# Two depthwise convolutions with group norms: border rows written three times, fetched with one transfer per half, and all bands of the second convolution ahead of its border products

## The reference

```python
# first layer: 5x5, 3x3 and 1x1 depthwise convolutions of the group-normed x, mixed by alpha
g = _gn(x)            # 32 groups of 3 channels, over 3*128*128 points of an image
x = x + alpha[0]*g + alpha[1]*dw1x1(g, w1) + alpha[2]*dw3x3(g, w3) + alpha[3]*dw5x5(g, w5)
# second layer: one 3x3 kernel for every channel, and a bias
g = _gn(x)
x = x + conv3x3(g, w) + b
```

## Time and profile before

| | |
|---|---|
| median of 3 runs | 431.48 us (428.29, 431.50, 431.48) |
| the profiled execution's own time | 432.64 us, of which the span in the trace is 430.8 us |
| mean granted clock of PE | 0.903 of full speed |
| busy in the span: PE, PE weight loads | 318.5 us (74%), 276.8 us (64%) |
| DVE, ACT, POOL | 318.1 us (74%), 304.1 us (71%), 262.3 us (61%) |
| DMA | 69.40 MB, mean 161 GB/s |
| chain that ended last, by engine | DVE 33%, DMA 21%, SP's queue 13%, ACT 13%, PE 9% |

### The profile page before, as it was taken

One profiled execution on the slowest core, in us unless ns is written; L12 is line 12 of the kernel. 1 busy time (PEld: TensorE's weight loads), 2 busy tenths in 40 slices (PEclk: granted clock), 3 DMA queues, 4 the chain that ended last, 5 costly groups with the idle time before them and its releaser, 6 DMA issues.

```text
span 430.8 us, 12547 instructions
## 1 busy us (share of the span) xinstructions
PE 318.5 (74%) x5206; PEld 276.8 (64%) x5206; DVE 318.1 (74%) x688; ACT 304.1 (71%) x372; POOL 262.3 (61%) x206
## 2 busy tenths in 40 slices
PE   2491586754986998679894998499848989898440
PEld 2361273643986798459883897389836989897220
DVE  7861899971886998399929994889649996779620
ACT  1407257089999699939995899759993999977320
POOL 6405055058788578827885588738882788865601
PEclk9997596995999899969996999889998999999685
DMA  6689488201687769676986788676868514731965
GB/s 151 169 174 204 129 188 169 73 3 41 159 200 164 199 177 210 158 189 202 199 194 171 198 184 202 161 214 173 189 163 223 145 41 118 201 97 28 264 173 146
DMA packets 112829, 69.40 MB, mean 161 GB/s; under 512 B 4540, under 2 KB 109892, under 8 KB 112772
## 3 DMA queue, kind: packets, MB, share of 16 engines
q1 hardware_dynamic: 106088, 65.31, 60.5%
q10 hardware_dynamic: 6684, 3.29, 3.3%
HBM read 41.10 MB, written 27.48 MB: 159 GB/s over the span
## 4 chain that ended last, share of the span: by engine, by line
DVE 33%; DMA 21%; SPq 13%; ACT 13%; PE 9%; issue 4%; ACTq 2%; POOL 2%; POOLq 0%; DVEq 0%
DVE xt L697 15%; DVE stats L641 13%; DMA xt<-in_x_dram 10%; PE ps L377 8%; DMA edge_scratch<-gnX 6%; ACT gn_f L551 5%; SPq L236 5%; ACT gnX L552 4%; ACT cross L561 3%; SPq L216 3%; DMA edge_scratch<-gnY 2%; SPq L250 2%; POOL gnX L864 1%; SPq L263 1%; ACTq L244 1%
## 5 line engine op out<-in xcount | busy, mean ns | idle before, releaser
L377 PE MATMUL ps<-gnX,band 64*64 64x512 f16 x2880 | 181.6, 397 | 29.9 <-DVE xt L697 18.1
L377 PEld LDWEIGHTS ps<-gnX,band 64*64 64x64 f16 x2880 | 161.1, 188 | 46.6 <-issue 40.2
L697 DVE SCALAR_TENSOR_TENSOR xt<-ps,unscale,xt 128x512 f32<-128x512 f32 (+1 forms) x194 | 143.8, 747 | 22.9 <-PE ps L377 20.1
L641 DVE BATCH_NORM_STATS2 stats<-xt 128x6 f32<-128x384 f32 x256 | 120.9, 546 | 45.6 <-DMA xt<-in_x_dram 44.9
L377 PE MATMUL ps<-gnY,band 64*64 64x512 f16 x1728 | 116.8, 414 | 33.7 <-DVE xt L697 33.7
L864 POOL TENSOR_TENSOR gnX<-gn_f,gnX 128x768 f16<-128x768 f32 x60 | 92.7, 1545 | 60.7 <-ACT gnX L552 60.7
L377 PEld LDWEIGHTS ps<-gnY,band 64*64 64x64 f16 x1728 | 97.9, 190 | 49.1 <-ACT gnY L552 23.0
L551 ACT ACTIVATE gn_f<-xt,g_add,g_mul 128x768 f32<-128x768 f32 x120 | 122.1, 1017 | 4.9 <-DVE g_add L681 4.3
L864 POOL TENSOR_TENSOR gnY<-gn_f,gnY 128x768 f16<-128x768 f32 x60 | 92.7, 1545 | 31.0 <-ACT gnY L552 31.0
L561 ACT ACTIVATE cross<-ps,unscale 64x512 f32<-64x512 f32 x94 | 64.2, 683 | 51.0 <-PE ps L377 49.4
L873 POOL TENSOR_TENSOR xt<-xt,cross 128x512 f32<-128x512 f32 x47 | 61.7, 1315 | 57.3 <-ACT cross L561 57.2
(11 more groups left out here) (78 smaller groups left out, 97.9 us busy)
## 6 DMA issues: line engine op xcount, KB each, us to landing
out_dram<-xt SPq DMA_DIRECT2D x56, 384.0 KB, 4.8
xt<-in_x_dram SPq DMA_DIRECT2D x48, 384.0 KB, 6.4
band<-diag_scratch SPq DMA_DIRECT2D x48, 160.0 KB, 3.0
haloX<-edge_scratch SPq DMA_DIRECT2D x32, 123.4 KB
xt<-in_x_dram SPq DMA_DIRECT2D x20, 192.0 KB, 4.3
xt<-in_x_dram ACTq DMA_DIRECT2D x12, 192.0 KB, 6.0
out_dram<-xt SPq DMA_DIRECT2D x12, 192.0 KB, 4.0
haloX<-edge_scratch SPq DMA_DIRECT2D x32, 61.7 KB
```

The source lines that it names most:

```text
L377: mm = nc.tensor.matmul(ps[to, c, half, :], weights(rows, half), moving(rows, half), start=first, stop=last)
L641: st = nc.vector.bn_stats(stats[:, q_of(at, i) % 2, at, b, e, :], flat[:, SUB * e:SUB * (e + 1)])
L697: ev = nc.vector.scalar_tensor_tensor(out=here, in0=ps[frm, c, half, :].rearrange("h (b w) -> h b w", b=NB), scalar=unscale[rows, at:at + ...
```

## The change

It has three parts. First, `edge_scratch` gets room for three parts instead of two, and `edges_out` writes the high part a second time, in a DMA of its own behind each one there was. Second, `edges_in` needs one transfer per half instead of two, since the three parts now lie in one piece; `halo_landed` and the counts on `edges_landed` follow. Third, PE does `conv(Y, ., 2)` ahead of `edge(Y, ., 0)` in every unit; before it did so only in the last. Line numbers in the changed kernel are shifted by a few.

```diff
-        edge_dram = [nc.dram_tensor(f"edge_scratch{s}", [2, 2, 2, 2, FAR[s], ROW], fp16, kind="Internal").ap() for s in (X, Y)]
+        edge_dram = [nc.dram_tensor(f"edge_scratch{s}", [2, 2, 3, 2, FAR[s], ROW], fp16, kind="Internal").ap() for s in (X, Y)]
...
         def halo_landed(n):
-            return 64 * (n // 2 + 1)
+            return 32 * (n // 2 + 1)
...
                         src = gn[s][row:row + 2, p, :, 1 - side, :, :, :].rearrange("r h b c w -> r h (b c w)")
-                        eng.dma_start(edge_dram[s][p, g, :, side, :, :].rearrange("h r e -> r h e"), src).then_inc(edges_landed[s], 16)
+                        eng.dma_start(edge_dram[s][p, g, 0:2, side, :, :].rearrange("h r e -> r h e"), src).then_inc(edges_landed[s], 16)
+                        eng.dma_start(edge_dram[s][p, g, 2, side, :, :], src[:, 0, :]).then_inc(edges_landed[s], 16)
                 else:
                     row = (0, R - 1)[side]
                     src = gn[s][row:row + 1, p, :, 1 - side, :, :, :]
-                    eng.dma_start(edge_dram[s][p, :, :, side, 0, :],
+                    eng.dma_start(edge_dram[s][p, :, 0:2, side, 0, :],
                                   bass.AP(src.tensor, src.offset, [[R * pitch, 2], [2 * ROW, 2], [1, ROW]]))\
                        .then_inc(edges_landed[s], 16)
+                    eng.dma_start(edge_dram[s][p, :, 2, side, 0, :],
+                                  bass.AP(src.tensor, src.offset, [[R * pitch, 2], [1, ROW]])).then_inc(edges_landed[s], 16)
...
         def edges_in(eng, s, i):
-            n = rows * len(taps)
-            eng.wait_ge(edges_landed[s], (64, 32)[s] * (i + 1))
+            n = 3 * rows * len(taps)
+            eng.wait_ge(edges_landed[s], (128, 64)[s] * (i + 1))
...
-                for at, parts in ((0, 2), (2, 1)):
-                    eng.dma_start(halo[s][R * g + at * n:R * g + (at + parts) * n, p, :, :, :]
-                                  .rearrange("r b c w -> r (b c w)")[:, 0:EDGE],
-                                  bass.AP(src.tensor, src.offset + taps[0], [[ROW, parts * rows], [1, len(taps)], [1, EDGE]]))\
-                       .then_inc(halo_in[s][p], 16)
+                eng.dma_start(halo[s][R * g:R * g + n, p, :, :, :].rearrange("r b c w -> r (b c w)")[:, 0:EDGE],
+                              bass.AP(src.tensor, src.offset + taps[0], [[ROW, 3 * rows], [1, len(taps)], [1, EDGE]]))\
+                   .then_inc(halo_in[s][p], 16)
...
                     conv(Y, i - LAG, 1)
-                    if i - LAG < LAST:
-                        edge(Y, i - LAG, 0)
                     conv(Y, i - LAG, 2)
-                    if i - LAG == LAST:
-                        edge(Y, i - LAG, 0)
-                    edge(Y, i - LAG, 1)
-                    edge(Y, i - LAG, 2)
+                    for c in range(CG):
+                        edge(Y, i - LAG, c)
```

## The result

The changed kernel takes 427.07 us (median of 20 runs, 422.7 to 431.2), the kernel before 430.52 us beside it (20 runs, 427.7 to 433.6). The ratio is 0.9896 with an interval of 0.9867 to 0.9925: 4.5 us less (3.2 to 5.7), where -4.8 was forecast. The total is right. The parts are not, as the rest shows: they were -10 and +5.5 where I had -7.0 and +2.2.

The account below looks back on a forecast made before the run. The prediction took a chain through SP's queue to bound the kernel, with the last load of x behind X's border rows. Terms: -7.0 + 1.5 + 1.2 + 0.2 - 0.7 = -4.8, giving 426.7 us (range 420.5 to 435.5).

Parts of the forecast that it names:

- Two fetches fewer: SP's queue ahead of the last load of x: 1.4 us freed in each of five load steps, -7.0 us.
- The landing behind the last write: Sign in load steps: X's border rows land about 4 us after their last write starts, not 4.9.
- Four writes more: X's border rows: last write starts 1.04 us later, mostly hidden by the queue of loads; 0.3 us five times, +1.5.
- Y's border rows and the first loads: Four turns between load steps: PE's order and Y's writes delay the first loads 0.3 to 1.5 us each; +1.2 taken.
- The stores' hold-up: SP's queue at Y's border-row writes: stores queued ahead would have drained by up to 1.2 us more when writes start later.
- The rival of no change: Hold-up of SP's queue by stores does not shrink, first loads start 1.5 us later per turn: 431.5 us, chance 0.22.
- Late stage: From about 333 us, without loads: PE's new order adds 0.2 us once, where this stage begins.
- ACT's wait for PE: Sign before ACT's first copy in store steps: 2 us longer each, 32 us in all instead of 23.9.
- The last unit: ACT's queue: four writes take 1.2 to 2.0 us more, the second fetch starts 2.3 us sooner; -0.7 us taken.
- The rival of the engines: Few DMA engines carry border rows; 60-row fetches spread better, speeding start and five loads: -8.9, 422.6 us, chance 0.18.
- The rival that was slower: X's border rows in load steps: landing follows its last write, so delays count in full: +6.9, 438.4 us, chance 0.15.

Follow-up runs that it names:

- taps outermost: The rows only kernel with X's 60 border rows per half fetched with the five taps as outermost dimension, border weights reordered to match: 444.05 us, ratio 1.0319 to before.
- rows only: The changed kernel with PE's old order put back, keeping the third part in the scratch and one fetch per half: 420.09 us, ratio 0.9764 to before.
- the fetch split again: The rows only kernel with every fetch cut in two again, 40 and 20 rows for X, keeping the new writes: 451.13 us, ratio 1.0468 to before.
- third part spread: The rows only kernel with X's third-part writes sent as eight one-partition transfers, each written as eight pieces: 428.33 us, ratio 0.9974 to before.
- order only: The kernel before with PE's new order alone and the old border rows: 435.35 us, ratio 1.0127 to before.
- the load ahead: Last batch's load issued before the fetch of X's border rows in load steps: on the changed kernel 420.63 us (0.9768), on rows only 421.73 us (0.9810).

## Why the prediction was right, and where it was not

*The total* was right: -4.8 forecast, -4.5 measured (ratio 0.9896), with the forecast at 426.7 us and the median at 427.07. It is so because two misses of about 3 us cancel. By the prediction's terms the rows were to give -7.0 + 1.5 - 0.8 (of the 1.2, what two writes more and two fetches fewer make in four turns) - 0.7 = -7.0, and PE's order +2.0 (4 x (1.7 - 1.2)) + 0.2 = +2.2. Measured apart: -10.2 and +5.5.

*Two fetches fewer, -7.0.* The step "one of 60 rows I take at the same price" was off: one takes 0.8 us (1.67 for two), so in issues the term is -5.6. In time it is -31 us for the fetches of X and Y, measured with the writes in place; the issues are the smaller part of it. What the term left out is the number of engines that share a fetch: by taps outermost alone it can carry 24 us. The landing behind the last write shortened in all four load steps that both chains show, by 0.5 to 1.1 us, as predicted. In the four turns rows only gains 1.4 us behind the first load and 0.3 ahead of it, where the terms give 1.1 and 0.2; most of the rest of its gain lies at the start.

*Four writes more, +1.5.* They take 0.25 to 0.29 us each, as assumed. What of them counts I had far too small: with the fetches as before they cost 20 us together with Y's (the kernel with the fetch split again), and four further issues still cost 1.4 us per load step (third part spread) where I let 0.3 through. I looked for the price in the wrong place. Behind the first load, where a later write was to join the same queue, the split kernel is 0.1 us slower per turn, so that argument stands. The price is ahead of the first load: I counted none of X's writes among the stores, and where SP's queue has no idle time before Y's rows they count in full. That the net of the rows was still near my sum is luck: the fetch gained as much more.

*Y's border rows and the first loads, +1.2.* Too small. Every link was there with its size (ACT's copy +2.1, the writes +1.8). The stores' hold-up drained in three turns of the changed kernel and not in the one shown above. The first loads leave 0.6 us later in the mean of the four turns (25.53, 25.06, 25.99 and 26.76 us behind the statistics, before 25.17, 25.63, 24.97 and 25.02), where I took 0.3 and had 1.5 as the upper end: +2.6 us instead of +1.2. The rival of no change named the one turn without draining; it does not decide. The +2.6 is less than the +5.5 measured for PE's order. In the trace of order only the five load steps take 4.0 us more, 1.8 of it in the first, for which I put nothing, and the store steps 0.55.

*PE's order elsewhere.* Late stage: +0.2 predicted; from root 15 on, order only and before take 94.99 and 94.97 us. That fits. ACT's wait for PE, 32 us predicted: 28.6 in order only, 23.1 in the changed kernel. Wrong: ACT itself arrives later, in the order-only step 7.9 us behind the statistics (240.80 less 6.37, less 226.57) instead of 5.9.

*The last unit, -0.7.* From the first write to the last fetch's issue it takes 9.86 us (401.33 to 411.19) instead of 8.79 (403.33 to 412.12), and the landing 3.87 instead of 4.31: +0.6. Four writes take ACT's queue 5.3 us (401.33 to 406.59), 3.3 us more than the two, where I gave 1.2 to 2.0:

```profile
401.33 1.19 ACTq L221 DMA_DIRECT2D edge_scratch<-gnY  x1
402.55 0.67 ACTq L224 DMA_DIRECT2D edge_scratch<-gnY  x1
403.25 1.69 ACTq L221 DMA_DIRECT2D edge_scratch<-gnY  x1
404.96 1.63 ACTq L224 DMA_DIRECT2D edge_scratch<-gnY  x1
410.32 1.61 ACTq L238 DMA_DIRECT2D haloY<-edge_scratch  x2
```

*The rival of the engines.* I gave it 0.18 as an alternative, -4.1 us on top of the forecast; as the packets show more engines at work on a fetch, it belonged into the sum. Root 2 comes at 43.32, 46.05, 46.95 and 49.15 us in the four kernels with the new rows and the old layout, and at 48.09, 50.60, 50.66 and 52.01 in the four with the old rows: 46.4 against 50.3, 4.0 us sooner in the mean, although single executions scatter by 6 us. With the 6.9 us of the load steps of rows only that makes -10.9, near the measured -10.2. Taps outermost shows that the shape of the fetch alone can carry such an amount. The other half of this rival, the writes on few engines, is not tested by any run.

*The rival that was slower* (the landing follows the last write) holds in one respect. Last write in the chain, and the fetch behind it, before and then changed:

```profile
255.98 5.24 DMA edge_scratch<-gnX
...
261.24 2.79 SPq L236 DMA_DIRECT2D haloX<-edge_scratch  x4
```

```profile
253.43 4.72 DMA edge_scratch<-gnX
...
258.17 1.68 SPq L238 DMA_DIRECT2D haloX<-edge_scratch  x2
```

Counted from the statistics (225.71 and 221.10) the last write starts at 32.3 instead of 30.3 us, and the landing comes at 37.1 instead of 35.5. The landing follows by three quarters there. From the first load to the statistics the changed kernel is 1.05 us faster per turn all the same, so the shorter fetch more than pays for it.

What stays open: how the 5.5 us of PE's order are made up, of which the four turns show 1.9 in the trace of order only; by which way a fetch on few engines makes the last load late; what spreading the writes would do; and why X's third part costs nothing once the fetch is whole, while Y's does. The best kernels with the whole result are rows only, 420.09 us, 2.4% below before and 1.3% below the changed kernel, and, within the noise, the two with the load ahead.

## What to carry to other kernels

Time the parts of a change apart even when the total came out as forecast: here a gain of 10 us had a loss of 5.5 us in it, and dropping PE's new order was worth as much as the best edit that was added to the change (the load ahead), each 1.3%. When transfers have few rows, look at how they are laid out, not only at how many are issued: the same 60 rows in another order of dimensions cost 5.7%. A wait that shrinks (34.7 to 25.9 us) tells what an engine no longer waits for, not what the kernel gains; count start times from a common event, such as one row per unit, and over all turns: the hold-up of the stores stands in one turn of four only. Before reading the time of a test, look in its trace whether the edit did what it was to do: the third part was never spread.

## What the hardware showed that I had not expected

- A transfer of 60 rows in five groups of twelve is issued faster than in twelve of five (median 775 against 1065 ns) and makes the kernel 24 us slower; at most 7 of its packets are under way at once instead of 14 to 16.
- A write of two partitions costs 0.26 us to issue, one of a single partition and half the bytes 0.28 us: the queue's time is per transfer here, not per byte. A contiguous row written as eight pieces in the program left as one packet of 3168 bytes.
- Root 2 comes at 43.32 us in rows only and at 49.15 in the changed kernel, which first differ in a product of Y, far behind it; among the 14 profiled executions it goes from 42.76 to 52.10. A single trace does not measure a change of the start.
- The store steps take 19.51 to 19.54 us in most kernels, from the one of 407.5 us of span to the one of 455.2: in the last of these the writes make the load step behind it longer, not the store step itself.
